# Four edits at once in a fused graph, attention and expert kernel: a block in halves, a bias by tiles, rows gathered earlier, a convolution's entry inside its neighbour's pass

## The chip, the cores and the metric

One NeuronCore of a Trainium2 chip runs the whole kernel in one launch. The metric is the device time of one execution in microseconds, lower is better. TensorE is called PE (its weight loads PEld), VectorE DVE, ScalarE ACT, GpSimd POOL, and SyncE, which here only issues transfers, SP.

## The reference, cut to what matters

The input is `x` (3125 rows of 256, float32) and 53,125 edges sorted by destination. Four residual blocks follow each other, each on the layer-normalised rows:

```
x = x + L0_gnn(layernorm(x))   # 3 x (mean over edges @ Wl + bl + h @ Wr, batch norm, relu): 256-512-512-256
x = x + L0_ffn(layernorm(x))   # slice attention: softmax over 64 slices in 8 heads, attention on 64 tokens
x = x + L1_gnn(layernorm(x))   # two hypergraph convolutions
x = x + L1_ffn(layernorm(x))   # 8 experts, top 2, layer norm, 256-1024-256 with exact gelu

def _hconv(x, W, b, src, dst, n):          # twice in L1_gnn, with _prelu between
    xt = x @ W
    m = segment_sum(xt[src], dst) * Binv[:, None]
    out = segment_sum(m[dst], src) * Dinv[:, None]
    return out + b
```

## The kernel before, in words

**The count table.** POOL adds the edges one by one, 128 per indirect transfer, into two tables of counts in device memory, `at_counts` and `odd_counts` (line 552). A group is 8 such transfers; even groups go to one table, odd groups to the other, 52 groups in all. DVE prepares the indices of all groups (lines 1050 to 1063) and does nothing else after them until all 52 are prepared. The two tables added are the adjacency, so that every sum over edges becomes a product on PE.

**Blocks and tiles.** Nodes are cut into `T = 25` tiles of 128 and `NB = 5` blocks of 640; the last block has 565 nodes. A block's columns of the table come as five chunks `q` of 128 x 3200 fp16 (819 kB each) into the buffer `ring`; PE has halves of a block as banks of 320 columns. Since the edges are sorted by destination, the groups of an early block land first; `block_releases` (lines 1028 to 1047) works out after how many groups each block's columns are complete, and SP waits for that number (`released`).

**Layer 0 of the graph network.** For each block, SP loads the five even and five odd chunks, DVE adds them (`sum_tables`, line 1162), PE multiplies (`aggregate`, lines 1754 and 1762: 10 products with a matrix of ones for the degrees and 40 others for each chunk), DVE divides by the degree (lines 1121 to 1137), PE applies `Wl` (line 1780), DVE adds and takes statistics (lines 1144, 1111), and ACT stores the summed chunks. The next layer starts after the batch norm of all five blocks (`bn_k`, line 1211). Block 4 is released only with the last group. On DVE the sums of block 4 stand behind all of block 3's work.

**The FFN.** A loop over tiles on all engines; DVE does the softmax, POOL only adds up `weight_sum` (line 598). Behind the loop POOL adds the output bias `bout` to all 25 tiles of `xrows` in one instruction (line 601), while DVE and PE compute the attention on 64 tokens (DVE 1292 to 1325, PE 1918 to 1944). Two products with a row of zeros (`zero_row`, PE 1878 and 1906) open and close the accumulation of the tokens. `wsquare` and `scale_across`, `scale_spread`, `scale_power` and `scale_back` find a power of two by which the fp16 pairs of the convolution are scaled.

**The convolutions.** An entry (`conv_rows`) turns each tile (PE 1970), multiplies it by the weight (PE 1977) and splits it into a high and a low fp16 part (ACT 855, DVE 1361). In the first entry the FFN's output products (PE 1951) run eight tiles ahead, with DVE 1334 and 1338 behind them and the normalising (DVE 999) in front. Then passes `c = 0..3` of five blocks each: 250 products a block on lines 2008 and 2009, with the tables `at` and `ad` in turn. Pass 1 ends in `rows2`, the hidden rows; the second entry starts when all of pass 1 is done, since its scale comes from the largest of the hidden rows (DVE 1434, `half_scale(4, T)`), and POOL copies each tile for it (line 609).

**The experts.** 32 chunks, three of 256 rows and one of 128 in turn. POOL gathers a chunk's rows (`gather_rows`, line 620), PE turns them (2069), and does the two products (2079 hidden, 2088 outputs); DVE adds bias and gate; POOL adds the rows into `x_sum` (line 642) and waits for that addition's landing before anything else. All this is in the order of POOL's program:

## Time and profile before

| | |
|---|---|
| three timed runs | 3054.23 us median (3053.55 to 3055.42) |
| profiled execution | 3055.43 us, span 3053.6 us |
| busy | PE 2275.3 us (75%), DVE 1314.2 (43%), POOL 888.4 (29%), ACT 375.8 (12%) |
| chain that ended last | PE 59%, POOL 16%, DVE 10%, issue 7%, DMA 5%, ACT 2% |
| largest lines of the chain | PE 1762 16%, PE 2008 8%, PE 2009 8%, POOL 552 8% and 7% |

The span is one execution from its first to its last instruction, and the timed run holds 1.8 us more. The kernel is a row of stages, each with its own limit: up to 624 us DVE and POOL work on the tables, up to 900 us layer 0 runs, the graph network ends at 1594 us, the FFN's loop at 1751 us, the convolutions run from 1815 to 2500 us, and the experts from about 2599 to 3036 us. A share of the whole says little of one stage. What an edit is worth is read from the wait that ends last in its stage.

### The profile page before, as it was taken

To read this page: it belongs to the slowest core of one execution; us is meant where nothing else is said; L and a number is where in the kernel's file an instruction comes from. 1 tells how busy PE (TensorE), PEld (TensorE's weight loads), DVE (VectorE), ACT (ScalarE), POOL (GpSimd) and SP (SyncE) were. 2 spreads that over 40 slices of the span, in tenths; PEclk is the share of its full clock that TensorE was granted. 3 is DMA by queue.
4 is the path that set the end of the run, shared out by engine and by line. 5 is a ranking of instruction groups with operands and counts; after the bars stand their busy time and mean duration, and the time that the engine had idled before them with its cause. 6 is when DMAs were issued, how large, how long until landed. Compare 5 with 4: busy or idle time off the path is not lost.

```text
span 3053.6 us, 39654 instructions
## 1 busy us (share of the span) xinstructions
PE 2275.3 (75%) x14187; PEld 1775.8 (58%) x14187; DVE 1314.2 (43%) x2799; ACT 375.8 (12%) x789; POOL 888.4 (29%) x638
## 2 busy tenths in 40 slices
PE   1033100069779999999988977999899995999997
PEld 1022100046557776778763456888688884788886
DVE  7899999954431111111127743113311667111111
ACT  0011000000015000004002202000210000222221
POOL 4888888878800000000011300000100001233332
PEclk6566555579989999999998969999999996999998
DMA  9943333398550999950460000444234434566665
GB/s 338 339 67 48 42 55 48 35 310 249 137 192 0 181 260 218 261 172 0 137 192 0 0 1 11 150 145 148 83 119 150 138 103 128 162 194 208 185 191 170
DMA packets 287137, 425.19 MB, mean 139 GB/s; under 512 B 165698, under 2 KB 222553, under 8 KB 286975
## 3 DMA queue, kind: packets, MB, share of 16 engines
q1 hardware_dynamic: 104895, 295.72, 29.9%
q10 hardware_dynamic: 109760, 108.33, 13.1%
q0 software_dynamic: 72400, 20.04, 7.8%
q8 instruction: 51, 0.84, 0.1%
q14 instruction: 31, 0.25, 0.0%
HBM read 306.57 MB, written 100.17 MB: 133 GB/s over the span
## 4 chain that ended last, share of the span: by engine, by line
PE 59%; POOL 16%; DVE 10%; issue 7%; DMA 5%; ACT 2%; DVEq 0%; ACTq 0%; SPq 0%; POOLq 0%
PE ps L1762 16%; PE ps L2008 8%; PE ps L2009 8%; POOL at_counts L552 8%; POOL odd_counts L552 7%; PE ps L2088 6%; PE ps L1780 4%; PE ps L1694 4%; PE ps L2079 4%; DMA x_sum<-harena 2%; PE ps L1951 2%; PE ps L1848 2%; DMA xrows<-odd_counts 1%; PE ps L1977 1%; DMA harena<-xn_rows,harena 1%
## 5 line engine op out<-in xcount | busy, mean ns | idle before, releaser
L2008 PE MATMUL ps<-harena,ring 128*128 128x257 f16 x2500 | 556.7, 275 | 3.7 <-DVE harena L1361 2.7
L2009 PE MATMUL ps<-harena,ring 128*128 128x256 f16 x2500 | 556.4, 274 | 0.0
L1762 PE MATMUL ps<-ring,harena 128*128 128x320 f16 (+1 forms) x4000 | 539.2, 297 | 1.4 <-ACT tarena L713 0.8
L1762 PEld LDWEIGHTS ps<-ring,harena 128*128 128x128 f16 x4000 | 391.9, 98 | 144.6 <-issue 3.1
L1056 DVE SCALAR_TENSOR_TENSOR late<-ring,ps 128x1024 f16<-128x1024 f32 x312 | 378.9, 1275 | 12.3 <-DMA ring<-key_rows 10.1
L552 POOL DMA_INDIRECT at_counts<-harena x208 | 330.7, 1590 | 110.0 <-issue 104.0
L552 POOL DMA_INDIRECT odd_counts<-harena x208 | 328.7, 1580 | 63.7 <-issue 61.8
L2008 PEld LDWEIGHTS ps<-harena,ring 128*128 128x128 f16 x2500 | 243.7, 97 | 43.2 <-DVE harena L1427 3.8
L2009 PEld LDWEIGHTS ps<-harena,ring 128*128 128x128 f16 x2500 | 243.2, 97 | 33.0
L1786 PE MATMUL ps<-ident,sc 128*1 128x128 f32 x8 | 2.1, 365 | 288.5 <-DVE sc L1004 288.5
L2088 PE MATMUL ps<-ring,harena 128*128 128x256 f32 x896 | 202.2, 384 | 7.8 <-ACT harena L902 6.6
L2079 PE MATMUL ps<-harena,ring 128*128 128x256 f32 (+1 forms) x1024 | 202.5, 357 | 1.2 <-DVE harena L1615 1.2
L2079 PEld LDWEIGHTS ps<-harena,ring 128*128 128x128 f32 x1024 | 178.0, 193 | 22.2 <-issue 1.6
L2088 PEld LDWEIGHTS ps<-ring,harena 128*128 128x128 f32 x896 | 169.0, 191 | 34.9 <-issue 13.5
L1137 DVE SCALAR_TENSOR_TENSOR feat<-ps,sc,late 128x640 f32<-128x640 f32 x30 | 26.5, 883 | 348.5 <-PE ps L1762 348.5
L577 POOL DMA_DIRECT2D wl<-L_ffn_W_out x1 | 0.7, 712 | 586.8 <-DVE feat L1137 586.8
L1786 PEld LDWEIGHTS ps<-ident,sc 128*1 128x1 f32 x8 | 0.4, 81 | 290.2 <-issue 284.0
L902 ACT ACTIVATE harena<-ps,harena 128x256 f32<-128x256 f32 (+1 forms) x256 | 114.4, 447 | 358.6 <-PE ps L2079 354.2
L1371 DVE TENSOR_SCALAR late<-ps 128x1 f32<-128x1 f32 x100 | 15.4, 154 | 325.0 <-PE ps L2009 325.0
L1780 PE MATMUL ps<-feat,wl 128*128 128x320 f32 x480 | 134.8, 442 | 18.3 <-DVE feat L1137 17.2
L609 POOL COPY feat<-tarena 128x256 f32 x25 | 9.8, 400 | 438.0 <-DVE tarena L1432 414.3
L642 POOL DMA_INDIRECT x_sum<-harena x56 | 89.1, 1590 | 145.1 <-DVE harena L1625 135.7
(382 smaller groups left out, 2620.1 us busy)
## 6 DMA issues: line engine op xcount, KB each, us to landing
ring<-at_counts SPq DMA_DIRECT2D x150, 800.0 KB, 4.5
ring<-L_ffn_W SPq DMA_DIRECT2D x64, 1024.0 KB, 5.5
ring<-ad_counts SPq DMA_DIRECT2D x50, 800.0 KB, 4.2
ring<-key_rows SPq DMA_DIRECT2D x52, 512.0 KB, 3.8
at_counts<-tarena ACTq DMA_DIRECT2D x5, 4000.0 KB, 15.0
odd_counts<-tarena ACTq DMA_DIRECT2D x5, 4000.0 KB, 27.2
xrows<-odd_counts SPq DMA_DIRECT2D x25, 800.0 KB, 8.3
at_counts<-ring ACTq DMA_DIRECT2D x25, 800.0 KB, 7.5
```

Of the source, the lines that this page charges most:

```text
L552: nc.gpsimd.indirect_dma_start(out=table, out_offset=bass.IndirectOffsetOnAxis(ap=eidx[:, c:c + 1], axis=0), in_=evalue[:, c:c + 1], in_of ...
L642: nc.gpsimd.indirect_dma_start(out=x_sum, out_offset=bass.IndirectOffsetOnAxis(ap=to_row[:, j:j + 1], axis=0), in_=yrow[c % 2][:, i, :], i ...
L902: nc.scalar.activation(hT[s][:, k, 0:n], ps[:, k % 4, 0:n], ACT.Gelu, bias=evc[s][:, k:k + 1]).then_inc(e_gelu, 1)
L1056: ins = V.scalar_tensor_tensor(out=ejunk[q], in0=krow[:, s, :], scalar=ekey[:, bass.ds(g + q, 1)], in1=weight_ps[:, GE - P - q * P:2 * GE ...
L1694: ins = M(ps[:, 4 + n % 4, 0:c], weights[:, d, fo * P:(fo + 1) * P], feat[:, d, h * HB:h * HB + c], start=(d == 0), stop=(d == 3))
L1762: ins = M(ps[:, 2 * f + h, 0:c], part[:, t, (2 * k + f) * P:(2 * k + f + 1) * P], chunk[q][:, s, h * HB:h * HB + c], start=(t == 0 and par ...
L1780: ins = M(ps[:, k + h, 0:HB], wl2[:, d, fo * P:(fo + 1) * P], feat[:, d, h * HB:(h + 1) * HB], start=(d == 0), stop=(d == nfi - 1))
L1848: return M(ps[:, i % 4, 0:F], feat[:, d, i * P:(i + 1) * P], wl3[:, d, :], start=(d == 0), stop=(d == 3))
L2008: M(ps[:, i, 0:F + 1], lhs, hh[:, t, 0:F + 1], start=(t == 0), stop=False)
L2009: ins = M(ps[:, i, 0:F], lhs, hl[:, t, :], start=False, stop=(t == T - 1))
L2079: ins = M(ps[:, k % 4, 0:n * P], w1e[s][:, d, k * P:(k + 1) * P], xeT[s][:, d, 0:n * P], start=(d == 0), stop=(d == 1))
L2088: ins = M(ps[:, 4 + s, i * F:(i + 1) * F], hT[s][:, k, i * P:(i + 1) * P], w2e[s][:, k, :], start=(k == 0), stop=(k == EK - 1))
```

## The change

It has four parts, and what they carry with them.

1. **The last block of layer 0 in halves** of 320 and 245 nodes. `block_releases` works out six numbers instead of five (one more comparison over the edges and one more counting instruction on DVE). SP loads each half of a chunk by itself (pieces of 640 bytes), DVE sums, divides and adds half by half, and PE does the half's aggregation and its products with `Wl`.
2. **Bias tile by tile.** POOL adds `bout` to one tile in each turn of the FFN's loop. The zero rows go. The convolution's two scales come from bounds on the weights (a reduction of the squares of both weight matrices by PE and DVE) and not from data, so both are there before the first entry. In the first entry DVE normalises tile t+1 before it adds the FFN's row t+8.
3. **Second entry inside the passes.** In pass 1 the hidden rows go straight to `urow`; block b's tiles are turned, multiplied and split between the products of block b+1, and those of block 4 in the first block of pass 2, with PSUM banks 5, 6 and 7.
4. **Expert rows ahead.** POOL gathers chunk c+3 right behind the issue of chunk c's additions, and waits for the landing afterwards.

The diff, cut to its core. SP and POOL:

```diff
-            for q in range(NB):
-                load_odd((NB - 1) * NB + q)
...
+            def load_half_even(q, h):
+                n = (NB - 1) * NB + q
+                if h == 0:
+                    sp.wait_ge(chunk_used[q], NB)
+                    sp.wait_ge(sum_out[(n - NB) % 2], 16 * ((n - NB) // 2 + 1))
+                sp.dma_start(chunk[q][:, :, h * HB:(h + 1) * HB], half_of(at, q, h)).then_inc(chunk_in[q], 16)
...
+            def load_half_odd(q, h):
+                m = (NB - 1) * NB + h * NB + q
+                sp.wait_ge(tables_summed, m - 1)
+                sp.dma_start(odd_half(m, h), half_of(odd, q, h)).then_inc(odd_in[m % 2], 16)
...
+            for h in range(2):
+                released(0, NB - 1 + h)
+                for q in range(NB):
+                    load_half_even(q, h)
+                released(1, NB - 1 + h)
+                for q in range(NB):
+                    load_half_odd(q, h)
...
                 for i in range(BT):
+                    r = bass.ds(b * BT + i, 1)
+                    pool.wait_ge(f_rows, b * BT + (i + 1))
+                    pool.nop(nofuse=True)
+                    nc.gpsimd.tensor_tensor(xrows[:, r, :], xrows[:, r, :], bout.unsqueeze(1), ALU.add).then_inc(f_bias, 1)
...
                     pool.nop(nofuse=True)
...
-            nc.gpsimd.tensor_tensor(xrows[:, :, :], xrows[:, :, :], bout.unsqueeze(1).to_broadcast([P, T, F]), ALU.add).then_inc(f_bias, 1)
...
             pool.wait_ge(r_dve, 4)
             for c in range(CHUNKS):
-                if c + 2 < CHUNKS:
-                    pool.wait_ge(e_tps, c + 1)
-                    gather_rows(c + 2)
...
+                if c + 3 < CHUNKS:
+                    pool.wait_ge(e_tps, c + 2)
+                    gather_rows(c + 3)
                 pool.wait_ge(y_added, 16 * sum(UNITS_OF[:c + 1]))
```

DVE's side of part 1, with its new functions:

```diff
+                step(V.scalar_tensor_tensor(out=eflt[:, 3, :], in0=eflt[:, 1, :], scalar=float((NB - 1) * BC + HB), in1=eflt[:, 3, :], op0=ALU.is_ge, op1=ALU.add))
+                for b in range(NR):
...
+                def sum_half(q, h):
+
+                    m = (NB - 1) * NB + h * NB + q
+                    dve.wait_ge(chunk_in[q], 16 * (NB + h))
+                    dve.wait_ge(odd_in[m % 2], 16 * (m // 2 + 1))
+                    own = chunk[q][:, :, h * HB:(h + 1) * HB]
+                    V.tensor_tensor(own, own, odd_half(m, h), ALU.add).then_inc(tables_summed, 1)
+
+                def aggregated_half(h):
+
+                    b, c = NB - 1, half_width(h)
+                    n0 = b * BC + h * HB
+                    own = deginv[:, n0:n0 + c]
+                    dve.wait_ge(deg, NB + h)
+                    step(V.tensor_scalar(own, ps[:, 4 + h, 0:c], 1.0, None, ALU.max))
+                    if h == 1:
+                        o.mark(V.memset(deginv[:, N:], 0.0))
...
+                        mine = tfeat[:, fo, n0:n0 + c]
+                        dve.wait_ge(ops, (b + h) * 4 + (fo + 2))
+                        V.tensor_tensor(mine, ps[:, 4 + 2 * (fo % 2) + h, 0:c], mine, ALU.add).then_inc(odone, 1)
+                        if fo >= 1:
+                            half_stats(h, fo - 1)
+                        if fo >= 2 and h == 1:
...
-                                sum_tables(NB - 1, q)
...
+                if l == 0:
+                    for h in range(2):
+                        for q in range(NB):
+                            sum_half(q, h)
+                        aggregated_half(h)
```

PE's side of part 1:

```diff
+                b, c = NB - 1, half_width(h)
...
+                for q in range(NB):
+                    pe.wait_ge(tables_summed, b * NB + h * NB + (q + 1))
+                    own = chunk[q][:, :, h * HB:h * HB + c]
+                    for j in range(BT):
...
+                        if t == 0 and h == 0:
+                            pe.wait_ge(agg[0][0], b * 2 + (f + 1))
+                        for part in (hh, hl):
+                            ins = M(ps[:, 2 * f + h, 0:c], part[:, t, f * P:(f + 1) * P], own[:, s, :],
+                                    start=(t == 0 and part is hh), stop=(t == T - 1 and part is hl))
+                        if t == T - 1:
+                            if h == 0:
+                                ins.then_inc(half_summed, 1)
+                            elif f == 0:
+                                ins.then_inc(first_summed, 1)
...
+            def mean_products_half(h):
+
+                mean, ops, odone = agg[0]
+                b, c = NB - 1, half_width(h)
+                pe.wait_ge(mean, (NB + h) * 2 + 2)
+                pe.wait_ge(degdone, NB + 1 + h)
+                for fo in range(4):
+                    pe.wait_ge(odone, (b + h) * 4 + (fo if fo >= 2 else 1) if h == 0 or fo >= 2 else b * 4 + 1)
+                    for d in range(2):
...
+            for h in range(2):
+                aggregate_half(h)
+                mean_products_half(h)
```

DVE's side of part 2:

```diff
-            V.memset(zero_row, 0.0).then_inc(f_dve, 1)
...
+                V.tensor_tensor(squares[k], matrix, matrix, ALU.mult).then_inc(c_square, 1)
...
+            V.tensor_reduce(wsquare, ps[:, 4, :].rearrange("p (k c) -> p k c", k=2), AX.X, ALU.max).then_inc(c_square, 1)
...
-            step(V.tensor_copy(amax[:, 0:1], wnorm[:, 0:1]))
-            V.tensor_reduce(scale_of(3)[:, 2:3], amax[:, 0:1], AX.X, ALU.max).then_inc(sc_col, 1)
...
+            step(V.tensor_tensor(bound[:, 1:2], bound[:, 1:2], wnorm[:, 0:1], ALU.add))
+            step(V.tensor_scalar(bound[:, 1:2], bound[:, 1:2], steepest, wnorm[:, 1:2], ALU.mult, ALU.mult))
+            step(V.tensor_scalar(bound, bound, 1e-30, None, ALU.max))
+            step(V.tensor_scalar(bound.bitcast(i32), bound.bitcast(i32), 0x7F800000, None, ALU.bitwise_and))
+            step(V.tensor_scalar(two_scales[:, :, 1], bound, 2.0 ** -13, None, ALU.mult))
+            V.reciprocal(two_scales[:, :, 0], two_scales[:, :, 1]).then_inc(sc_ready, 1)
             dve.wait_ge(f_pe, 7)
...
-            scale_power(3)
             V.memset(conv_halves[0][0][:, :, F:F + 2], 1.0).then_inc(c_ones, 1)
-            dve.wait_ge(f_bias, 1)
-            scale_back(3)
+            dve.wait_ge(f_bias, T)
...
                 r = t + AHEAD
-                if t < T:
-                    conv_normal(t, t % BT)
+                if t + 1 < T:
+                    conv_normal(t + 1, (t + 1) % BT)
                 if r < T:
                     add_ffn(r)
                 if r <= T:
...
-                    first_low(t - 2, (t - 2) % BT)
+                    conv_low(t - 2, (t - 2) % BT, 0)
```

Parts 2 and 3 on DVE and PE:

```diff
-                        step(V.tensor_scalar(negrows, zrows, 0.0, slope, ALU.min, ALU.mult))
-                        V.scalar_tensor_tensor(out=rows2[:, blk, :], in0=zrows, scalar=0.0, in1=negrows, op0=ALU.max, op1=ALU.add).then_inc(c_h, 1)
-                        dve.wait_ge(c_h, b + 1)
-                        o.mark(V.tensor_reduce(amax[:, blk], rows2[:, blk, :], AX.X, ALU.max, apply_absolute_value=True))
...
+                edge_means(b, 1)
+                step(V.tensor_scalar(negrows_of[1], zrows_of[1], 0.0, slope, ALU.min, ALU.mult))
+                V.scalar_tensor_tensor(out=urow, in0=zrows_of[1], scalar=0.0, in1=negrows_of[1], op0=ALU.max, op1=ALU.add).then_inc(c_h, 1)
...
+            edges_out(0)
+            hidden_block(0)
+            with o.loop_from(1, NB, 3 * BT + 1) as b:
+                second_entry(b * BT - BT)
+                hidden_block(b)
+            second_entry(T - BT)
+            edges_out(2)
...
+                      start=isinstance(t, int) and t == 0, stop=isinstance(t, int) and t == T - 1)
...
-            for k in range(2):
-                M(ps[:, 4 + k, :], zero_row[:, 0:P], zero_row, start=False, stop=True)
...
+            def second_entry(b, t0):
+
+                def between(n):
+                    if n == BT - 1:
+                        pe.wait_ge(c_h, b + 1)
+                    i = (n - (BT - 1)) // 2
+                    if n >= BT - 1 and (n - (BT - 1)) % 2 == 0 and i <= BT:
+                        if i >= 1:
+                            conv_product(t0 + (i - 1), i - 1, 1)
+                        if i < BT:
+                            conv_turn(t0 + i, i, 1)
+                return between
...
+            def conv_sums(b, c, between=nothing_between):
...
+                    if c == 2 and isinstance(b, int):
+                        pe.wait_ge(c_low, T + (q * BT + BT + 1))
...
+                        if n % BT == BT - 1:
+                            between(q * BT + n // BT)
...
+            conv_sums(0, 1)
+            with pe.Fori(1, NB) as b:
+                conv_sums(b, 1, second_entry(b - 1, b * BT - BT))
+            conv_sums(0, 2, second_entry(NB - 1, T - BT))
+            with pe.Fori(1, NB) as b:
+                conv_sums(b, 2)
```

How the instructions stand on the engines. On DVE, at the last block of layer 0, before (line 1162 is the sum of a chunk's two tables, 1121 to 1137 the degree and the division, 1144 and 1111 the addition and the statistics):

```order
L1111 BN_STATS bn_st<-tarena 128x6 x4
L1162 TENSOR_TENSOR ring<-ring,xrows 128x3200 x5
L1121 TENSOR_SCALAR late<-ps 128x640
L1125 MEMSET late 128x75
L1127 RECIPROCAL late<-late 128x565
L1137 SCALAR_TENSOR_TENSOR feat<-ps,late 128x640 x2
L1144 TENSOR_TENSOR tarena<-ps,tarena 128x640 x2
```

And now:

```order
L1147 BN_STATS bn_st<-tarena 128x6 x4
L1206 TENSOR_TENSOR ring<-ring,xrows 128x5x320 x5
L1214 TENSOR_SCALAR late<-ps 128x320
L1218 RECIPROCAL late<-late 128x320
L1228 SCALAR_TENSOR_TENSOR feat<-ps,late 128x320 x2
L1233 TENSOR_TENSOR tarena<-ps,tarena 128x320 x2
L1243 BN_STATS bn_st<-tarena 128x6
L1233 TENSOR_TENSOR tarena<-ps,tarena 128x320
L1243 BN_STATS bn_st<-tarena 128x6
L1233 TENSOR_TENSOR tarena<-ps,tarena 128x320
L1243 BN_STATS bn_st<-tarena 128x6 x2
L1206 TENSOR_TENSOR ring<-ring,xrows 128x5x320 x5
```

The five sums of the second half stand behind the whole of the first half's division, addition and statistics. On PE, the second convolution's entry stood by itself between pass 1 and pass 2 (1970 turns a tile, 1977 multiplies it):

```order
L1970 MATMUL ps<-ident,feat 128x128 x4
L1977 MATMUL ps<-wr,feat 128x256 x2
L1970 MATMUL ps<-ident,feat 128x128 x2
L1977 MATMUL ps<-wr,feat 128x256 x2
L1970 MATMUL ps<-ident,feat 128x128 x2
```

Now it stands between the products of a block (2151 and 2152 are what 2008 and 2009 were, 2108 and 2101 what 1977 and 1970 were):

```order
L2151 MATMUL ps<-harena,ring 128x257
L2152 MATMUL ps<-harena,ring 128x256
L2105 REGISTER_ALU
L2108 MATMUL ps<-wr,feat 128x256 x2
L2101 MATMUL ps<-ident,feat 128x128 x2
L2151 MATMUL ps<-harena,ring 128x257
L2152 MATMUL ps<-harena,ring 128x256
```

Six such places stand in each of five blocks, ten pass products of each of the two lines apart. On POOL, in the FFN's loop and at its end, before:

```order
L598 TENSOR_TENSOR late<-late,harena 128x512
L593 REGISTER_ALU
L593 COMPARE_AND_BRANCH
L601 TENSOR_TENSOR xrows<-xrows,harena 128x6400
L605 UNCONDITIONAL_BRANCH
```

And now:

```order
L633 ISA
L633 TENSOR_TENSOR xrows<-xrows,harena 128x256
L637 TENSOR_TENSOR late<-late,harena 128x512
L631 REGISTER_ALU
L633 ISA
```

The one addition over all tiles has become one of 256 columns a turn, in front of the turn's addition to `weight_sum`.

## Rows read from the trace of the kernel before

**Rows 1.** PE in time, last block of layer 0: start, duration, instruction, idle before.
```profile
851.88 2.52 PE L1754 MATMUL ps<-ring,ones 128*128 128x320 f16 x10 [25.87 <-issue]
...
861.69 4.98 PE L1762 MATMUL ps<-ring,harena 128*128 128x320 f16 x40
...
886.42 8.88 PE L1780 MATMUL ps<-feat,wl 128*128 128x320 f32 x32 [1.68 <-DVE feat L1137]
```

**Rows 2.** DVE in time, the same block.
```profile
826.79 1.66 DVE L1111 BATCH_NORM_STATS2 bn_st<-tarena 128x6 f32<-128x320 f32 x4
849.96 3.76 DVE L1162 TENSOR_TENSOR ring<-ring,xrows 128x3200 f16<-128x3200 f16 x2 [21.51 <-DMA xrows<-odd_counts]
...
900.15 0.16 DVE L1211 TENSOR_TENSOR bn_k<-vec,bn_k 128x4 f32<-128x4 f32 x1
```

**Rows 3.** SP's queue in time, loads of that block.
```profile
828.37 2.49 SPq L438 DMA_DIRECT2D ring<-at_counts  x5
843.11 17.26 SPq L444 DMA_DIRECT2D xrows<-odd_counts  x5
```

**Rows 4.** PE in time, entry of the FFN.
```profile
1617.12 3.78 PE L1878 MATMUL ps<-harena 1*128 1x512 f32 x4 [2.98 <-DVE harena L1258]
```

**Rows 5.** DVE in time, the same stretch.
```profile
1618.35 0.32 DVE L996 RECIPROCAL ln_r<-ln_s 128x25 f32<-128x25 f32 x1 [0.29 <-ACT ln_s L680]
1622.71 0.69 DVE L1288 COPY harena<-ps 128x512 f32<-128x512 f32 x1 [4.04 <-PE ps L1879]
```

**Rows 6.** PE in time, behind the FFN's loop.
```profile
1750.67 1.98 PE L1906 MATMUL ps<-harena 1*128 1x512 f32 x4
...
1763.46 0.47 PE L1919 MATMUL ps<-harena 1*64 1x64 f32 x2
...
1796.70 3.78 PE L1951 MATMUL ps<-harena,tarena 128*128 128x256 f32 x8 [2.05 <-DVE harena L1325]
```

**Rows 7.** POOL in time, the same stretch.
```profile
1749.66 13.69 POOL L601 TENSOR_TENSOR xrows<-xrows,harena 128x6400 f32<-128x6400 f32 x1
```

**Rows 8.** DVE in time, in the loop's last turns and behind it.
```profile
1727.96 0.69 DVE L1278 TENSOR_REDUCE harena<-harena 128x8 f32<-128x512 f32 x1 [0.43 <-ACT harena L827]
...
1755.54 8.08 DVE L1294 TENSOR_SCALAR harena<-harena 64x512 f32<-64x512 f32 x1
...
1768.51 0.68 DVE L1302 TENSOR_TENSOR harena<-ps,harena 64x512 f32<-64x512 f32 x1
1774.66 1.88 DVE L1305 COPY harena<-ps 64x512 f32<-64x512 f32 x3 [5.47 <-PE ps L1927]
```

**Rows 9.** Waits of the first convolution's entry: total us, times, longest.
```profile
PE ps L1970 <- DVE feat L999: 15.6, 17, 1.7
```

**Rows 10.** Stretches: us, busy us of PE, PEld, DVE, ACT, POOL, clock, DMA share.
```profile
1751.73:1796.70 44.97, 28.78 (x134) 19.39 (x132) 24.18 (x24) 3.03 (x4) 11.61 (x1) 0.54 0.00 1
1815.52:1898.02 82.50, 62.05 (x286) 47.28 (x287) 35.88 (x117) 21.52 (x54) 0.00 (x0) 1.00 0.00 1
2173.57:2222.19 48.62, 33.85 (x154) 25.16 (x155) 18.33 (x40) 18.96 (x50) 9.78 (x25) 0.93 0.05 17
2222.19:2359.00 136.81, 136.19 (x1220) 118.34 (x1221) 14.94 (x62) 9.68 (x21) 0.00 (x0) 0.99 0.43 139
```

**Rows 11.** Waits of the experts' stage: total us, times, longest.
```profile
POOL harena L620 <- DMA x_sum<-harena: 130.5, 25, 7.8
...
PE ps L2069 <- DMA harena<-xn_rows,harena: 16.7, 7, 2.7
```

**Rows 12.** POOL in time, in the edges' transfers.
```profile
782.19 1.55 POOL L552 DMA_INDIRECT at_counts<-harena  x1 [0.30 <-issue]
```

**Rows 13.** One line of DVE: duration min/median/max in ns, starts, form.
```profile
L1033 DVE SCALAR_TENSOR_TENSOR late<-harena,ones x5: 681/691/691, 136.3 to 139.2; 104x512 f16<-104x512 f32 x5
```

**Rows 14.** PE in time, second convolution's entry.
```profile
2185.98 1.03 PE L1977 MATMUL ps<-wr,feat 128*128 128x256 f32 x4
```

**Rows 15.** DVE in time, behind pass 1.
```profile
2175.81 1.49 DVE L1432 SCALAR_TENSOR_TENSOR tarena<-harena 128x1280 f32 x1 [0.16 <-DVE harena L1431]
```

338 lines of the change are left out of this document (181 added, 157 removed).

## The prediction

> **What bounds the kernel now.** I read the page's slices first: PE is at 9 tenths or more in most slices from layer 0 on, DVE and POOL only before it. So an edit pays where PE stands still, or where PE does work that can go. The chain of waits then says PE 59%, POOL 16%, DVE 10%. I went on to the four places that the change touches, each with the timeline of the engines that wait there.
>
> At the last block of layer 0 PE is idle for 25.87 us and starts at 851.88 [rows 1]. DVE had finished block 3 at 826.79 + 1.66 = 828.45 and then waited 21.51 us for the odd table's chunks, whose loads SP issued at 843.11 [rows 2, 3]. So the last group's landing sets this block, and its end (the batch norm at 900.31) sets layer 1. At the FFN's entry PE works on zero rows and the slice bias, and DVE's copy waits 4.04 us for it, to 1622.71, though the statistics were ready at 1618.35 + 0.32 = 1618.67 [rows 4, 5]. Behind the loop PE does zero rows, and a DVE instruction of 64x512 takes 8.08 us while POOL's one long addition of 13.69 us runs [rows 6, 7, 8]. In the first convolution's entry PE loses 15.6 us in 17 waits for the normalising [rows 9]. The second entry is a stretch of 48.62 us with PE busy for 33.85 of them, in front of five pass blocks that fill PE (136.19 of 136.81) [rows 10]. In the experts' stage PE waits 16.7 us in 7 waits for gathered rows, behind a POOL that waits 130.5 us for additions to land, up to 7.8 at a time [rows 11].
>
> **The change part by part.**
>
> *(1) Last block in halves.* The first half needs only nodes under 2880. 48,958 edges lead to those, by groups of 1024 that is 47.8, so 48 of the 52 groups. POOL issues the first transfer of group 48 at 782.19 [rows 12], so the first 48 are out by then, some 46 us before DVE is free. The first half is bound by DVE's 828.45. A sum of a whole chunk takes 1.88 (two in 3.76) [rows 2], of 320 of 640 columns 0.94. 40 of PE's products took 4.98 [rows 1]. Half of them are 320 wide and half 245, 282.5 in the mean. Less the last one's own tail of some 0.16 that is 0.1205 each, so 0.136 at 320 wide and 0.105 at 245. The half is 125 products: from 829.5 about 17.0, to 846.5. Division for 320 columns and its product with the sums about 0.9 exposed, because the reciprocal needs only the degrees, which come before the last 20 products. Products with `Wl`: 16 of 0.277 (8.88 for 32 [rows 1]) are 4.4; DVE is done at about 852.7. The last group ends about where it did, and the loads of the second half can stand from 843.11 on. DVE's sums of the second half begin at 853.6, the third one waits for an odd load whose buffer came free with the first; I put 2 us of pacing there. PE: 853.7 + 125 x 0.105 = 866.8, with little pacing 867.1. Then 0.7 for the division, 3.8 for 16 narrower products, and the same tail as now: 895.3 (886.42 + 8.88) to 900.31 is 5.0. That gives 876.6 in place of 900.31, a gain of 23.7. Bounds: 27 with no pacing at all; 15 if each half load takes as long as a whole one does today (843.11 to the first sum at 849.96 is 6.85 us) and half the second half's chunks wait in turn.
>
> *(2) The release numbers.* Two more instructions on DVE of the kind of 0.69 [rows 13] and a settling between them: +1.6, since DVE's work on the groups stands in front of everything in this stage. Bounds 1.2 and 3.
>
> *(3) FFN entry.* Without zero rows (3.78 [rows 4]) and the memset in front, the slice bias is done before the statistics are. DVE's copy then starts at 1618.7 in place of 1622.71, and a little under half a microsecond of memset leaves its path: -4.5. Bounds 3.5 and 5.5.
>
> *(4) Tail of the FFN.* PE's zero rows of 1.98 go [rows 6]. With POOL's long addition gone, DVE's 8.08 should be what a 64x512 operation takes in the same view, 0.68. DVE would then be at its 1768.51 operation some 7 us earlier; PE, which it waits for too, ends line 1919 at 1763.93, less 1.98 is 1761.95. So 1762.05 in place of 1768.51, -6.45. In return PE gets the squares' products: 8 records at this clock took 3.78 [rows 6], of which the 1.88 of DVE's three copies [rows 8] is cover: +1.8 with rounding. Net -4.7. Bounds 2 and 8. The 8.08 falls into POOL's 13.69 (1749.66 to 1763.35) and ends 0.27 behind it [rows 7, 8]. The Trainium skill, "SBUF — State Buffer", section "Who interferes with whom", says that VectorE and GpSimd share a port pair as an exclusive lock, which `tensor_scalar` can want and which a `tensor_tensor` with both inputs in SBUF contends for too; by that rule, the trace agrees, the stall goes, but the rule also speaks against the new place of the bias (rival B).
>
> *(5) First entry.* DVE normalises one tile earlier, so that PE's 15.6 us of waits [rows 9] mostly go; DVE is busy for only 35.88 of 82.50 us there [rows 10]. I leave 1.4 (a wait for the first tile): -14.2. Bounds 8 and 15.6.
>
> *(6) Second entry inside the passes.* The 48.62 us go. PE's own work of the entry, 33.85 busy [rows 10], comes back between the products of blocks that fill PE. It holds about 2 us of scale and start that don't return. The floor is 28: a tile's product took 1.03 for its four records [rows 14], 26 for 25 tiles, and at least 2 for the turns that don't overlap. I take 31. Net -17.6; bounds -12 (36 with switches) and -21 (28). What hides the rest: ACT and DVE have room: they are busy for 9.68 and 14.94 of five blocks' 136.81, and the entry brings them 18.96 and 18.33 [rows 10]. The new wait for `c_h` stands ahead of PE's turn of the next block's tiles: queued behind it are all products of that block. DVE ended the hidden rows' last instruction at 2175.81 + 1.49 = 2177.30 [rows 15], 3.7 after pass 1's last product at 2173.57, and the turn stands behind 50 products of 0.11, or 5.5 us, so the wait should cost nothing.
>
> *(7) Experts.* The gather of chunk c+3 goes out before the additions' landing rather than behind it. Seven waits of about 2.4 (16.7 [rows 11]) fall to a total of about 1: -15.7. Bounds: -16.7 and 0, should the gather queue up behind the additions.
>
> *(8) What the tilewise bias costs in the loop.* POOL's addition is 13.69 / 25 = 0.55 a tile [rows 7]; DVE, which sets the loop's pace, has 0.43 idle in a turn [rows 8]. I take +2; bounds 0 and 12.
>
> Sum: -23.7 + 1.6 - 4.5 - 4.7 - 14.2 - 17.6 - 15.7 + 2.0 = -76.8. The profiled span is 3053.6, so 2976.8. The run around it took 1.8 more, 2978.6; the median of the timed runs stands 1.2 below the profiled run, which gives 2977.4. I say 2977.
>
> **The rivals.**
>
> *A: the halves are bound by their loads.* Pieces of 640 bytes rather than 1280, ten more transfers, and sums that wait for a buffer two back. For it: today the odd loads of this block already come out over 17.26 us for five of them, since each needs a buffer that a sum has left [rows 3]. Against: half of the data is there early. A gain of 15 to 19 in term 1 in place of 23.7: about 2984. A page bears on this: "DMA: Bandwidth & Descriptors", section "Measured (HBM→SBUF, 128 partitions, SWDGE, issued from GpSimd)" in the Trainium skill gives 341 GB/s for 1 MB and 138 for 64 KB and advises 1 MiB and more; a half chunk is between these. No run here shows such halves.
>
> *B: POOL and DVE in each other's way in the FFN loop.* POOL's 0.55 a tile could hold DVE's instruction each turn. For it: the 8.08 us. Against: the hold is one short instruction per turn, and 0.43 of idle time takes most. If all of 0.55 x 25 = 13.7 counts instead of my 2: about 2988.
>
> *C, the other side: slower than before.* Five blocks of a pass take 136.81 us at a granted clock of 0.99 [rows 10], which is TensorE's 2.4 GHz. Now tiles' turns and short products, each waiting for ACT's copies and DVE's splits, come in between. If PE stands still often enough in them that the clock falls to 1.2 GHz, as it is near in 1751.73 to 1796.70 (0.54, PE busy 64%), then these blocks take up to 136.8 more; the net is slower than before once this happens in over 76.8 / 136.8 = 56% of them, and with all it is about 3114. Against it: in 2173.57 to 2222.19 the same work by itself, busy 70%, had 0.93, and the first entry, busy 75%, 1.00.
>
> *D: the entry stalls the passes.* The turns wait on ACT's copy and the splits on DVE, in the order of PE's program. With one turn bank (5) and twenty products of 0.11 (136.81 / 1250 [rows 10]) between two steps, a stall of 0.6 us at each of the 30 places would undo term 6 (17.6): about 2995. For it: the entry by itself had PE idle for 14.8 of 48.62 us [rows 10]. Against: those twenty products are 2.2 us, and ACT and DVE together were busy for 37.3 us over 25 tiles in the stretch by itself, 1.5 a tile [rows 10].
>
> *E: the first half is not released earlier* (the number comes out at 52 groups): term 1 is then nothing, about 3001.
>
> **How the numbers follow.** My forecast 0.70; A 0.10; B 0.08; D 0.07; E 0.02; C 0.03. The likeliest case's own range is 2963 to 2990 (terms near their bounds on one side for two or three of them). The range of 8 in 10 goes to B and D on the upper side and a little further, and to all of terms 5 to 7 at their better bounds on the lower: 2960 to 3002. A measurement of this kernel can tell about 0.2%, 6 us, from no change. All cases but C lie more than 50 us below 3054: faster 0.96, same 0.01, slower 0.03.
>
> **What the profile after would show.** Right: PE's idle time before the last block gone or under 3 us, the five sums of the first half at 828 to 847, `bn_k` at about 878; DVE's first copy in the FFN right behind the statistics; no instruction of 64x512 above 1 us behind the loop; no group of waits for line 999's successor in the first entry; pass 2 beginning where pass 1 ends, with five blocks of 33 to 34 us in place of 27.4, at a clock near 1; PE's waits for gathered rows under 2 us in all. Wrong: sums of the second half each behind a load of 4 us or more (A); FFN turns over 4.8 us (B); a clock near 0.5 in the five blocks (C); idle time at the ten-product steps (D).

## The result and the profile after

| | before | after |
|---|---|---|
| timed runs, median | 3054.82 us (3053.55 to 3062.61) | 2974.23 us (2973.31 to 2975.66) |
| ratio of the fast runs | | 0.9729, 95% interval 0.9708 to 0.9751 |
| profiled execution, span | 3053.6 | 2972.6 |
| PE busy | 2275.3 | 2250.0 |
| chain: PE, POOL, DVE | 59%, 16%, 10% | 64%, 0%, 19% |

The forecast was 2977. Four runs of each kernel stand behind the ratio. To see where the 81.0 us of span went, I took the same instruction in both profiles at each border of a stage (start times in us; the last column is how much longer or shorter the stage before that border became):

| landmark | before | after | stage's change |
|---|---|---|---|
| batch norm of layer 0 | 900.1 | 884.4 | -15.7 |
| batch norm of layer 2 | 1591.7 | 1576.6 | +0.6 |
| FFN, copy of the slice bias | 1622.7 | 1603.2 | -4.4 |
| FFN, last softmax product | 1747.5 | 1734.0 | +6.0 |
| attention, `slT` | 1768.5 | 1746.5 | -8.5 |
| first product of pass 0 (line 2009, now 2152) | 1898.1 | 1858.6 | -17.5 |
| last product of pass 3 | 2524.8 | 2461.0 | -24.3 |
| first turn of the experts | 2596.8 | 2532.7 | -0.3 |
| last turn of the experts | 3020.2 | 2939.6 | -16.5 |

**The last block of layer 0.** PE's timeline after (start, duration, instruction, idle before), the counterpart of [rows 1]:

```profile
831.42 0.87 PE L1907 MATMUL ps<-ring,ones 128*128 128x320 f16 x5 [3.48 <-DVE ring L1206]
...
851.21 4.57 PE L1935 MATMUL ps<-feat,wl 128*128 128x320 f32 x16 [0.98 <-DVE feat L1228]
858.06 0.70 PE L1907 MATMUL ps<-ring,ones 128*128 128x245 f16 x5 [2.27 <-DVE ring L1206]
...
876.89 3.57 PE L1935 MATMUL ps<-feat,wl 128*128 128x245 f32 x16 [1.10 <-DVE feat L1228]
```

The 25.87 us of idle time have become 3.48, and the first half's `Wl` products are over before the second half starts. DVE's sums, against [rows 2]:

```profile
830.30 1.87 DVE L1206 TENSOR_TENSOR ring<-ring,xrows 128x1600 f16<-128x1600 f16 x2
834.69 0.99 DVE L1206 TENSOR_TENSOR ring<-ring,xrows 128x1600 f16<-128x1600 f16 x1 [2.52 <-DMA xrows<-odd_counts]
836.67 0.99 DVE L1206 TENSOR_TENSOR ring<-ring,xrows 128x1600 f16<-128x1600 f16 x1 [0.99 <-DMA xrows<-odd_counts]
839.16 0.99 DVE L1206 TENSOR_TENSOR ring<-ring,xrows 128x1600 f16<-128x1600 f16 x1 [1.50 <-DMA xrows<-odd_counts]
...
857.02 1.89 DVE L1206 TENSOR_TENSOR ring<-ring,xrows 128x1600 f16<-128x1600 f16 x2
863.64 0.99 DVE L1206 TENSOR_TENSOR ring<-ring,xrows 128x1600 f16<-128x1600 f16 x1 [4.73 <-DMA xrows<-odd_counts]
867.37 0.99 DVE L1206 TENSOR_TENSOR ring<-ring,xrows 128x1600 f16<-128x1600 f16 x1 [2.73 <-DMA xrows<-odd_counts]
871.94 0.99 DVE L1206 TENSOR_TENSOR ring<-ring,xrows 128x1600 f16<-128x1600 f16 x1 [3.58 <-DMA xrows<-odd_counts]
...
884.35 0.16 DVE L1296 TENSOR_TENSOR bn_k<-vec,bn_k 128x4 f32<-128x4 f32 x1
```

and SP's queue, against [rows 3]:

```profile
790.44 27.53 SPq L478 DMA_DIRECT2D ring<-at_counts  x5
818.64 17.43 SPq L483 DMA_DIRECT2D xrows<-odd_counts  x5
836.73 5.47 SPq L478 DMA_DIRECT2D ring<-at_counts  x5
850.58 14.44 SPq L483 DMA_DIRECT2D xrows<-odd_counts  x5
```

The first half's even loads are issued from 790.44 on and its first two odd loads from 818.64, ahead of DVE's first sum at 830.30; the other three odd loads wait for a buffer, and their sums for them (2.52, 0.99 and 1.50 us). The second half's odd loads are issued at 850.58, where before all of them went out from 843.11: the last group has landed 7.5 us later. Yet the first sum of the second half, at 857.02, has no idle time in front of it. It follows DVE's own work on the first half, and not the last group. The last three sums then wait 4.73, 2.73 and 3.58 us for a load each.

**The FFN.** DVE's copy of the bias follows the statistics at once (before it waited 4.04 us, [rows 5]), and behind the loop the instruction that took 8.08 us [rows 8] takes 0.41:

```profile
1603.22 0.69 DVE L1372 COPY harena<-ps 128x512 f32<-128x512 f32 x1
```

```profile
1740.10 0.41 DVE L1378 TENSOR_SCALAR harena<-harena 64x512 f32<-64x512 f32 x1
1740.54 3.35 DVE L1379 RECIPROCAL harena<-harena 64x512 f32<-64x512 f32 x1
...
1746.53 0.68 DVE L1388 TENSOR_TENSOR harena<-ps,harena 64x512 f32<-64x512 f32 x1 [0.73 <-PE ps L2051]
```

**The convolutions and the experts.** Stretches after, against [rows 10]: the first entry; a stretch that is mostly pass 1's first block, which carries no entry; and a stretch of the blocks behind it, which carry the second entry (us; busy us of PE, PEld, DVE, ACT, POOL; clock; DMA share; GB/s).

```profile
1793.89:1858.49 64.60, 58.20 (x286) 48.76 (x287) 35.86 (x117) 19.60 (x54) 0.00 (x0) 1.00 0.00 1
1994.00:2028.00 34.00, 33.95 (x311) 29.66 (x309) 10.43 (x35) 1.90 (x4) 0.00 (x0) 1.00 0.47 157
2028.00:2158.00 130.00, 130.00 (x1110) 113.88 (x1108) 37.80 (x109) 15.37 (x40) 0.00 (x0) 1.00 0.38 122
```

PE is busy without a gap where the entry stands between the products, at a granted clock of 1.00. The last instruction of the hidden rows comes every 32.84 us there and came every 27.41 before (DVE 1432, before). The fifth block with an entry, pass 2's first, takes 32.85:

```profile
2092.19 1.49 DVE L1513 SCALAR_TENSOR_TENSOR feat<-tarena 128x1280 f32<-128x1280 f32 x1
...
2125.03 1.49 DVE L1513 SCALAR_TENSOR_TENSOR feat<-tarena 128x1280 f32<-128x1280 f32 x1
```

In the experts' stage the 7 waits of 16.7 us [rows 11] are one of 5.1 at the start, and POOL's 130.5 us behind landings are 22.6 (us in total, times, longest):

```profile
POOL x_sum L669 <- DMA x_sum<-harena: 22.6, 6, 4.8
...
PE ps L2214 <- DMA harena<-xn_rows,harena: 5.1, 1, 5.1
```

### The profile page after: what moved, and what is told of

It reads as the page before. It is cut to its first block, busy times and chain, and to the rows that moved or that the text cites. A ratio compares the mean times of both kernels' runs of the same rounds, so it can differ in the third digit from the quotient of the medians.

```text
span 2972.6 us, 39530 instructions
## 1 busy us (share of the span) xinstructions
PE 2250.0 (76%) x14177; PEld 1767.3 (59%) x14177; DVE 1308.8 (44%) x2804; ACT 375.3 (13%) x789; POOL 891.0 (30%) x637
## 4 chain that ended last, share of the span: by engine, by line
PE 64%; DVE 19%; issue 7%; DMA 5%; ACT 2%; ACTq 2%; DVEq 1%; POOL 0%; SPq 0%
PE ps L1853 16%; PE ps L2151 8%; PE ps L2152 8%; PE ps L2233 7%; PE ps L2224 7%; DVE late L1092 6%; PE ps L1785 4%; PE ps L1871 4%; DVE ring L1092 4%; DMA odd_counts<-tarena 3%; DMA xrows<-odd_counts 2%; PE ps L1984 2%; PE ps L2085 2%; PE ps L2108 2%; ACTq L700 1%
## 5 line engine op out<-in xcount | busy, mean ns | idle before, releaser
L1853 PE MATMUL ps<-ring,harena 128*128 128x320 f16 x3800 | 512.7, 297 | 1.4 <-ACT tarena L743 0.8
L1853 PEld LDWEIGHTS ps<-ring,harena 128*128 128x128 f16 x3800 | 372.0, 98 | 138.7 <-issue 3.1
L1092 DVE SCALAR_TENSOR_TENSOR late<-ring,ps 128x1024 f16<-128x1024 f32 x312 | 379.0, 1276 | 12.5 <-DMA ring<-key_rows 10.4
L2233 PEld LDWEIGHTS ps<-ring,harena 128*128 128x128 f32 x896 | 167.6, 190 | 39.2 <-issue 17.7
L1871 PE MATMUL ps<-feat,wl 128*128 128x320 f32 x448 | 125.8, 442 | 16.3 <-DVE feat L1173 15.3
L1785 PE MATMUL ps<-feat,wr 128*128 128x320 f32 (+1 forms) x480 | 130.5, 429 | 0.0
## 6 DMA issues: line engine op xcount, KB each, us to landing
at_counts<-tarena ACTq DMA_DIRECT2D x5, 4000.0 KB, 15.5
odd_counts<-tarena ACTq DMA_DIRECT2D x5, 4000.0 KB, 27.3
```

Of the source, the lines that this page charges most:

```text
L1092: ins = V.scalar_tensor_tensor(out=ejunk[q], in0=krow[:, s, :], scalar=ekey[:, bass.ds(g + q, 1)], in1=weight_ps[:, GE - P - q * P:2 * GE ...
L1785: ins = M(ps[:, 4 + n % 4, 0:c], weights[:, d, fo * P:(fo + 1) * P], feat[:, d, h * HB:h * HB + c], start=(d == 0), stop=(d == 3))
L1853: ins = M(ps[:, 2 * f + h, 0:c], part[:, t, (2 * k + f) * P:(2 * k + f + 1) * P], chunk[q][:, s, h * HB:h * HB + c], start=(t == 0 and par ...
L1871: ins = M(ps[:, k + h, 0:HB], wl2[:, d, fo * P:(fo + 1) * P], feat[:, d, h * HB:(h + 1) * HB], start=(d == 0), stop=(d == nfi - 1))
L2233: ins = M(ps[:, 4 + s, i * F:(i + 1) * F], hT[s][:, k, i * P:(i + 1) * P], w2e[s][:, k, :], start=(k == 0), stop=(k == EK - 1))
```

## Experiments

Eleven variants of the changed kernel ran, and the kernel before once more. Two theories stood at the start: that each part did what the landmarks say of its stage, and that parts lean on each other, so that the sum came out right by chance.

**Part 1 undone.** The last block whole again, the six release numbers kept:

```diff
-            for h in range(2):
-                released(0, NB - 1 + h)
+            released(0, NB)
...
-                        for q in range(NB):
-                            sum_half(q, h)
-                        aggregated_half(h)
+                aggregated(NB - 1, LAST)
```

> Changed kernel with the last block of layer 0 whole again (the six release numbers stay, so DVE's groups end as in the changed kernel). Theory 1 (the halves are worth 17.7 us, as the landmarks of the two profiles say: batch norm of layer 0 done 15.8 us earlier, with 1.9 us more in front of it): 2974.2 + 17.7 = about 2992, batch norm at about 902. Rival (the halves are worth the forecast 23.7, and some other part of the change hides 6 us of it): about 2998.

Measured: 2997.89 us (2995.95 to 2998.95), 23.7 above the changed kernel, with the batch norm at 906.0. In the profiles that is 21.6 later than 884.4, not 17.7. So the rival was nearer: the halves are worth 22 to 24 us beside this kernel, as forecast, and something ahead of them costs some 6. (The profiles lie 24.5 apart at their end; 2.9 of that is the stretch behind the FFN's loop, where this kernel had the lower clock, see term 4.) Another count says the same: from the end of the last group of transfers to the batch norm it took 57.3 to 58.4 us in the four profiles with a whole block and 34.6 to 37.5 in the eight with halves and two odd buffers.

**The sixth release number as well.** The same kernel with five numbers (the minus lines are the changed kernel's):

```diff
-NR = NB + 1
+NR = NB
...
-                o.settle()
-                step(V.scalar_tensor_tensor(out=eflt[:, 3, :], in0=eflt[:, 1, :], scalar=float((NB - 1) * BC + HB), in1=eflt[:, 3, :], op0=ALU.is_ge, op1=ALU.add))
                 for b in range(NR):
```

> Changed kernel with the last block whole and only five release numbers, as before the change. Theory 1 (the sixth number's two instructions put VectorE 2.3 us later, which shifts its sums against GpSimd's transfers and costs up to 6 us at the last group): last group at 842, batch norm at 900 to 901, 2992. Rival (the last group's end only scatters): last group at 845 to 848, 2996 to 2998.

Measured: 2995.80 us (2994.69 to 2996.39), last group at 843.3, batch norm at 900.6. In the profile the sixth number costs 5.4 us, in the medians 2.1.

**The kernel before, once more.**

> The kernel before, profiled once more, to see how far its landmarks move from run to run. If the end of the last group at 841.7 was typical, it ends within 1 us of that again, and the changed kernel's 846.7 to 849.0 is an effect of the change. Rival (GpSimd's waits for landings at 680 to 690 scatter by themselves): it ends anywhere in 841 to 847.

Measured: 3055.59 us (3051.50 to 3087.85, 8 runs). The last group ended at 844.2, not 841.7, and the batch norm stood at 902.1. So this landmark scatters by 2.5 us in one and the same kernel. But the shift is more than scatter: the three profiles of kernels with five numbers have the last group at 841.7, 843.3 and 844.2, all eleven with six numbers at 846.7 to 849.0, and the means are 4.5 apart. DVE is through with the groups' indices at 623.90 before and at 626.26 after, 2.36 later. A wait of POOL, for the tables to be cleared, ends at 688.2 or 688.3 in all three kernels with five numbers and at 689.7 to 690.4 in all eleven with six, here before and after:

```profile
688.28 1.55 POOL L552 DMA_INDIRECT at_counts<-harena  x1 [7.65 <-issue]
```

```profile
689.92 1.55 POOL L586 DMA_INDIRECT at_counts<-harena  x1 [12.44 <-issue]
```

That is 1.6 of the 7.3 us between 841.7 and 849.0.

Where the other 5.7 come from, the profiles show too. POOL's transfers last 1.55 us, except some (after):

```profile
829.09 1.55 POOL L586 DMA_INDIRECT at_counts<-harena  x1 [0.30 <-issue]
830.95 1.75 POOL L586 DMA_INDIRECT at_counts<-harena  x1 [0.31 <-issue]
833.00 1.55 POOL L586 DMA_INDIRECT odd_counts<-harena  x1 [0.30 <-issue]
834.86 2.25 POOL L586 DMA_INDIRECT odd_counts<-harena  x1 [0.30 <-issue]
837.41 1.68 POOL L586 DMA_INDIRECT odd_counts<-harena  x1 [0.30 <-issue]
839.39 2.18 POOL L586 DMA_INDIRECT odd_counts<-harena  x1 [0.30 <-issue]
```

DVE's sums stood at 830.30 to 832.17 (two of them), 834.69 to 835.68, 836.67 to 837.66 and 839.16 to 840.15 (the fence of DVE's sums above). A transfer that starts while a sum is running ends 1.43 us after that sum's end: 834.86 lasts 0.70 longer with 0.82 of the sum still to run, 839.39 lasts 0.63 longer with 0.76 to run. A transfer that starts within 0.04 us of the sum's start isn't lengthened. From 620 to 850 us this holds in both kernels: before, the transfers that began inside a sum lasted 12.2 us longer in all, after 15.4, and the other 88 and 87 lasted longer by 0.02 and 0.01 in all. From POOL's wait at 688 or 690 to the last group there is nothing but transfers and their gaps of 0.30, so what lengthens them comes out at the end: 7.1 us before, 12.7 after. The sums of the first half, which now run beside the last group's transfers, make 1.6 of the difference. The rest is where each sum happened to meet a transfer: 7.1 to 9.6 in the three profiles with five numbers, 10.5 to 12.8 in the eleven with six.

**Is it the sum itself?** Idle sums for DVE, with one-input reductions of the same length in turn, in a stretch where it waits:

```diff
+                            for k in range(12):
+                                if k % 2 == 0:
+                                    step(V.tensor_tensor(junk, junk, junk, ALU.add))
+                                else:
+                                    step(V.tensor_reduce(junk[:, 0:4], ..., AX.X, ALU.max))
```

> Changed kernel with twelve idle instructions for VectorE between its sums of block 3 and its wait for the products (from 786 on): six sums of 128x3200 with two inputs in on-chip memory, and in turn with them six reductions of 128x1600 with one. Theory 1 (a VectorE instruction with two inputs there holds GpSimd's indirect transfers up, one with a single input does not): each transfer that a sum overlaps lasts 2 to 3.2 us in place of 1.55, those beside the reductions 1.55; the last group ends 4 to 8 us later. Rival (the sums hold GpSimd up because they go with loads and stores of the same chunks): all transfers there last 1.55.

Measured: one run, 2979.23 us; every transfer beside them lasted 1.55. This run settles nothing, and its profile shows why (DVE, then POOL):

```profile
790.54 1.82 DVE L1257 TENSOR_TENSOR xrows<-xrows 128x3200 f16<-128x3200 f16 x1
792.40 1.82 DVE L1259 TENSOR_REDUCE xrows<-xrows 128x4 f16<-128x1600 f16 x1
794.26 1.82 DVE L1257 TENSOR_TENSOR xrows<-xrows 128x3200 f16<-128x3200 f16 x1
```

```profile
790.51 1.55 POOL L586 DMA_INDIRECT at_counts<-harena  x1 [0.30 <-issue]
792.37 1.55 POOL L586 DMA_INDIRECT at_counts<-harena  x1 [0.31 <-issue]
794.23 1.55 POOL L586 DMA_INDIRECT at_counts<-harena  x1 [0.30 <-issue]
```

A sum and a reduction take 3.72 us together and two transfers with their gaps as well, so five of the six sums began 0.03 us behind a transfer's start and were over when the next began; the first began 0.02 us ahead of one, which is too little as well. The reductions began 0.03 us behind a transfer each, so they were never put to the test either.

The fourteen profiles answer the question without this kernel. Count as inside what starts at least 0.05 us after the start of DVE's instruction and 0.13 us before its end. In all profiles 334 transfers started inside a DVE instruction with two inputs in SBUF, the on-chip memory beside PSUM: 259 in the chunks' sums, the others before 380 us in work that has nothing to do with the chunks, the counting of the release numbers among it. Each ended 1.43 us after that instruction's end, within 0.02 us. And 3667 started inside instructions with one input in SBUF or none (statistics, reciprocals, products' sums out of PSUM): they lasted 1.55 to 1.58 us. One reciprocal, after:

```profile
813.11 4.15 DVE L1163 RECIPROCAL late<-late 128x640 f32<-128x640 f32 x1
```

```profile
814.24 1.55 POOL L586 DMA_INDIRECT odd_counts<-harena  x1 [0.30 <-issue]
816.10 1.55 POOL L586 DMA_INDIRECT odd_counts<-harena  x1 [0.30 <-issue]
```

So it is not the loads and stores that go with a sum. Two inputs are not the only case: 18 transfers that started inside the normalising (a `tensor_scalar` from SBUF to SBUF) were held in the same way, and the first transfer of each kernel, beside a copy out of PSUM, lasted 1.74, which isn't explained.

**Four buffers for the odd halves.** Each odd buffer has room for two halves, so four loads can be under way:

```diff
-            return runs(odd_chunk[m % 2], a=BT)[:, :, h * HB:(h + 1) * HB]
+            r = m // 2 % 2
+            return runs(odd_chunk[m % 2], a=BT)[:, :, r * HB:(r + 1) * HB]
...
-                sp.wait_ge(tables_summed, m - 1)
+                sp.wait_ge(tables_summed, m - 3 if m >= NB * NB - NB + 4 else min(m - 1, NB * NB - NB))
```

> Changed kernel with four half-wide buffers for the odd table's halves instead of two, so that four of these loads can be under way. Theory 1 (the second half is late mostly because the last group lands 7.3 us later than before, and a smaller part by the 4.7, 2.7 and 3.6 us that DVE's sums wait for their odd load): DVE's sums follow each other more closely, PE's second half ends some 4 us earlier, 2970. Rival A of the prediction (the loads pace the halves, all 6 us missing are theirs): 2968 or less. Third: the transfers share one line rate and the wait only moves: 2974.

Measured: 2972.46 us (2971.25 to 2972.84), batch norm at 879.8, 4.6 earlier. The first sum of the first half stood at 828.84 here, though, and at 830.30 in the changed kernel, which these buffers have no part in. The second half's sums, against 857.02 to 871.94 above:

```profile
855.21 3.78 DVE L1208 TENSOR_TENSOR ring<-ring,xrows 128x1600 f16<-128x1600 f16 x4
861.46 0.99 DVE L1208 TENSOR_TENSOR ring<-ring,xrows 128x1600 f16<-128x1600 f16 x1 [2.47 <-DMA xrows<-odd_counts]
```

From the first sum of the second half to the batch norm it took 24.5 us, against 27.3 with two buffers (26.6 to 28.3 in the eight kernels that have two, 24.5 in the other one with four). So waiting for buffers cost about 3 us; the medians give 1.8 of it.

**The bias, three ways.** In one piece behind the loop, as before:

> Changed kernel with the output bias in one GpSimd instruction behind the loop again. Theory 1 (GpSimd's additions in the FFN's loop cost 5.95 us through the port that it shares with VectorE, and the long one held VectorE for about 7 us behind the loop): loop ends 6 us earlier, the 64x512 instruction takes 8 us again, net +0 to +2: 2974 to 2976. Rival (the tilewise bias is nearly free, the tail's stall all that counts): 2980.

Tile by tile, but behind the loop:

```diff
-                    r = bass.ds(b * BT + i, 1)
-                    pool.wait_ge(f_rows, b * BT + (i + 1))
-                    pool.nop(nofuse=True)
-                    nc.gpsimd.tensor_tensor(xrows[:, r, :], xrows[:, r, :], bout.unsqueeze(1), ALU.add).then_inc(f_bias, 1)
...
+            with pool.Fori(0, NB) as b:
+                for i in range(BT):
+                    r = bass.ds(b * BT + i, 1)
+                    nc.gpsimd.tensor_tensor(xrows[:, r, :], xrows[:, r, :], bout.unsqueeze(1), ALU.add).then_inc(f_bias, 1)
```

> Changed kernel with the 25 short additions of the bias moved behind the FFN's loop, beside the attention's serial chain. Theory 1 (an addition of 0.55 us can hold VectorE for at most its own length, and the chain there is mostly waiting): loop 6 us shorter, tail at most 2 us longer, 2968 to 2970. Rival (25 additions in a row hold VectorE like one long one): 2974 to 2977.

And not at all:

> Changed kernel without the output bias's addition anywhere (this part of the computation is left out). Theory 1 (the additions stretch VectorE's instructions in the FFN's loop): the loop's turns go from 4.9 back to 4.7 us, 5.9 us less, 2968. Rival (the loop is longer for another reason, the order of the weight sums or the clock): 2974, turns of 4.9 us.

Measured: 2973.80 us (2972.28 to 2977.79), 2967.74 (2965.72 to 2982.35) and 2983.47 (2965.43 to 2987.22). The loop, from the copy of the bias to the last softmax product, took 130.8 us in the changed kernel and 124.6, 124.7 and 124.8 in these three, where before it had 124.8. So the additions inside the loop cost 6.0 us. From there to `slT` it took 21.3 us with the long addition, as before (21.0), and its 64x512 instruction lasted 8.35 again; with the short ones behind the loop it took 16.1, and without any 16.2. So the medians with the bias in one piece (2973.80) and tile by tile in the loop (2974.23) are the same: what the new place gave behind the loop it cost in the loop. Only the third place is better. In 17 to 20 turns DVE's groups read as follows, the changed kernel first, then the one without the bias (busy us, mean ns):

```profile
L1355 DVE TENSOR_TENSOR harena<-harena 128x512 f32<-128x512 f32 x19 | 15.5, 813 | 0.7
...
L1033 DVE TENSOR_SCALAR feat<-xrows,ln_mv,ln_r 128x256 f32 x19 | 11.4, 599 | 0.0
```

```profile
L1351 DVE TENSOR_TENSOR harena<-harena 128x512 f32<-128x512 f32 x20 | 13.9, 693 | 0.7
...
L1029 DVE TENSOR_SCALAR feat<-xrows,ln_mv,ln_r 128x256 f32 x17 | 6.9, 409 | 0.0
```

693 ns have become 813, and 409 have become 599: 0.31 us a turn, of which the idle time takes a part. They are the two instructions that POOL's addition stands beside, here in one turn (DVE, then POOL, whose own addition of 0.55 lasts 1.24):

```profile
1711.75 0.69 DVE L1355 TENSOR_TENSOR harena<-harena 128x512 f32<-128x512 f32 x1
1712.36 0.82 DVE L1033 TENSOR_SCALAR feat<-xrows,ln_mv,ln_r 128x256 f32 x1
```

```profile
1711.78 1.24 POOL L633 TENSOR_TENSOR xrows<-xrows,harena 128x256 f32 x1
```

The last kernel's median needs a word. In its profile, and in the profile of the second, layers 1 and 2 took 707.3 and 705.9 us in place of 692.3. PE waits there for ACT once, 14.0 us in the second kernel and 21.1 in place of 5.7 in the last one, where ACT's instruction stands behind the 125 transposing transfers of ACT's own program: their last starts at 1358.5, in the changed kernel at 1278.4. The bias has no instruction there, their fastest runs are 2965.4 and 2965.7, and the kernel before shows a smaller case in its second profile (698.3 against 691.6). What makes these transfers late in some executions stays open.

**The normalising in its old place.**

> Changed kernel with the normalising of tile t in its old place, behind nothing and ahead of the row t+8 only in its own turn. Theory 1 (the order alone removed PE's 15.6 us of waits): waits of about 15 us for the normalising come back in the first entry, 2989 to 2990. Rival (the scale that is there beforehand did part of it: the entry was 18.8 us shorter, not 14): only 10 to 12 come back, 2985.

Measured: 2993.59 us (2992.34 to 2994.18), +19.4. From `slT` to the first product of pass 0 it took 129.6 us, as before (129.6), against 112.1. PE's waits are those of [rows 9] again:

```profile
PE ps L2100 <- DVE feat L1033: 15.6, 17, 1.7
```

The order alone makes all of this stage's gain; the scale that is there beforehand adds none that could be seen.

**The entry's steps in one piece.**

```diff
-                    if n >= BT - 1 and (n - (BT - 1)) % 2 == 0 and i <= BT:
+                        for i in range(BT + 1):
```

> Changed kernel with the second entry's steps of a block of tiles in one piece, behind the 50th product of the next block, rather than spread over it. Theory 1 (spreading hides the copies and splits of ACT and VectorE, not PE's own 5.4 us a block): each tile's product now waits for its copy, some 1.2 to 1.7 us each, 25 times: +30 to +42, 3004 to 3016. Rival (the overlap with the passes is worth little, PE's work is all that counts): 2974 to 2980.

Measured: 3000.54 us (2996.61 to 3002.80), +26.3. The four passes took 626.3 us, against 602.4 spread out and 626.7 and 625.2 in two profiles of before. So all that the new place gives depends on the spreading: a block with the entry in one piece took 37.75 us, spread out 32.84. PE, at one of the pieces:

```profile
2034.80 0.38 PE L2101 MATMUL ps<-ident,feat 128*128 128x128 f32 x2
2035.95 1.13 PE L2108 MATMUL ps<-wr,feat 128*128 128x256 f32 x4 [0.76 <-ACT feat L879]
```

**The gathering in its old place.**

> Changed kernel with the experts' rows gathered in the old order, behind the landing of the additions. Theory 1 (this order alone made PE's 7 waits of 2.4 us): PE waits 16.7 us again, 2974.2 + 16.5 = about 2991. Rival (part of the 16.4 us that the stage lost comes from elsewhere, the clock for one): +10 to +12, 2985.

Measured: 2990.52 us (2984.26 to 2994.54), +16.3. The profiled run is the fastest of the four; in it the experts' stage takes 418.5 us, 11.7 more than in the changed kernel, and in the two profiles of before 423.3 and 420.7. PE's waits are back (the longest, at the start, the changed kernel has too):

```profile
POOL harena L648 <- DMA x_sum<-harena: 128.2, 27, 6.8
...
PE ps L2212 <- DMA harena<-xn_rows,harena: 19.0, 8, 5.2
```

**Both improvements together.**

> Changed kernel with both: the 25 bias additions behind the FFN's loop, and four half-wide buffers for the odd table's halves. Theory 1 (the two are in different stages and add up: -6.5 and -1.8 in medians, up to -4 by the batch norm's landmark): 2964 to 2966. Rival (the earlier end of layer 0 is given back in the next layer): 2967 to 2968.

Measured: 2966.46 us (2965.00 to 2972.51, 5 runs), 7.8 us below the changed kernel and 0.9702 of before (0.9667 to 0.9737). Its batch norm stands at 880.0 and its loop takes 124.8 us, so neither gives the other's back. It has the lowest median and the fastest run of all; that it beats the one with the bias alone (2967.74, fastest 2965.72) is within their scatter.

## Why the prediction was right, and which of its terms were not

The direction, the mechanism of each of the four parts and the time (2977 against 2974.23) were right, but the sum (-76.8 against -81.0) is better than its terms are. No run puts the zero rows back (term 3 and a part of term 4); what they cost is read from the landmarks alone.

- **(1) Halves, -23.7.** Beside the whole block with the same six numbers they measured -23.7 in medians and -21.6 in profiles. The forecast, though, was counted from the kernel before, with the last group in its old place. Counted so, terms 1 and 2 came to -15.7 together and not to -22.1. The half's work was put too short: the batch norm ended at 884.51, not 876.6. DVE began 1.9 us later than the forecast had it (830.30); from there to the second half's first sum it took 26.7 in place of 25.2, and from there on 27.5 in place of 23.0. The step that was mis-sized is the pacing by the odd loads. The text allowed 2 us for it and the sum took only 0.3 of them (866.8 to 867.1); four buffers took about 3 out. That is rival A's mechanism at a part of its size.
- **(2) Release numbers, +1.6.** The two instructions put DVE's groups 2.36 us later, and the last group of the kernels with six numbers ends 4.5 later in the mean. What was missed is that instructions of DVE hold POOL's transfers. In a kernel with a whole block this goes straight to the batch norm (906.0 against 900.6). In the changed kernel the second half's first sum hardly waited for the last group (no idle time ahead of the first two sums in seven of the ten profiles with halves, 0.14 to 0.38 us in the other three), so there it is mostly DVE's late start that counts. In medians the sixth number costs 2.1.
- **(3) FFN entry, -4.5.** Measured -4.4.
- **(4) Tail, -4.7.** `slT` came 8.5 earlier instead of 6.45. In that stretch the changed kernel's PE had a clock of 0.88; the kernels with a clock of 0.68 there took 15.5 us in place of 12.5. So 3 us of it come and go with the clock. The 8.08 us stall went, as forecast, and came back with the long addition (8.35).
- **(5) First entry, -14.2.** Measured -17.5. The residue of 1.4 that I left didn't stay. The waits that are back in the kernel with the old order are 15.6 us, so 1.9 of the 17.5 has no row of its own.
- **(6) Second entry, -17.6.** Measured -24.3 from the first profile of before and -22.8 from its second (four passes in 626.7, 625.2 and now 602.4 us): in the first, a stretch of the last pass had the clock at 0.86, and part of that came back behind it. The step that was mis-sized is the price of PE's work. I added the durations of groups (1.03 us for four records) where the next record starts after 0.87. The entry costs 5.43 us a block, 27.15 in all, and not 31; my floor of 28 was none. Another 1.3 us is the first block behind the separate entry, which took 29.10 us at a clock of 0.94 in both profiles of before, where the blocks behind it take 27.8: the forecast had no term for it. The wait for the hidden rows cost nothing, and the clock stayed at 1.00, so rivals C and D didn't come.
- **(7) Experts, -15.7.** Measured -16.5.
- **(8) Bias in the loop, +2.** Measured +6.0: rival B in nearly half its size. The idle 0.43 us of a turn stood ahead of another instruction than the two that were held, and only part of the 0.31 us could be taken from it.

Terms 4 to 7 were too small by 14 us and terms 1, 2 and 8 too favourable by 10. That the two nearly cancel was luck, and with it that the time came out within 3 us.

## What to carry to other kernels

When work moves between other work of the same engine, price it by the distance of the starts of its instructions, not by their durations, and check that it is spread: in one piece the same steps gave nothing. Before work goes to GpSimd because it is idle, look at which VectorE instructions will run beside it; the right place for 25 small additions was not the loop that VectorE bounds but the serial chain behind it. And where a stage waits for the last of a long row of transfers, count what lengthens each of them.
